# The keep and neg flags of a segment-maximum loop, loaded apart and the second one asked for three steps later

## The reference

```python
def _L2_gnn_ref(x, edge_index, edge_attr, W1, b1, W2, b2):
    rol, col = (edge_index[0], edge_index[1])
    e_feat = jnp.concatenate([x[rol], x[col], edge_attr], axis=-1)
    h = jax.nn.relu(e_feat @ W1 + b1)
    v = h @ W2 + b2
    x_cand = jax.ops.segment_max(v, col, num_segments=num_nodes)
    return jnp.maximum(x_cand, x[:, -v.shape[-1]:])
...
edge_index = jnp.stack([src, dst])
x = _layernorm(x + _L0_gnn_ref(x, src, dst, ...), axis=-1)
x = _layernorm(x + _L1_gnn_ref(x, edge_index, 3), axis=-1)
x = _layernorm(x + _L2_gnn_ref(x, edge_index, edge_attr_32, ...), axis=-1)
x = _layernorm(x + _L3_gnn_ref(x, edge_index), axis=-1)
```

## Time and profile before

| what | value |
|---|---|
| median of three runs | 13235.58 us |
| span of the profiled execution | 14030.5 us |
| the profiled execution's own time beside its span | not recorded, only the span is |
| the judging in it, 7445 to 12045 us | 4600 us |
| attention and count, 350 to 5270 us | 4920 us |
| two propagations, 5620 to 7300 and 12300 to 14030 us | 1680 and 1730 us |

### The profile page before, as it was taken

How to read it: one execution, slowest core, us unless ns; L and a number is a source line. 1 busy time by engine, 2 the same in 40 slices (tenths; PEclk the granted TensorE clock), 3 DMA queues, 4 the chain that set the end, 5 groups by cost and what they waited for, 6 DMA issues and landing times. The chain is left out here.

```text
span 14030.5 us, 252646 instructions
## 1 busy us (share of the span) xinstructions
PE 7954.3 (57%) x99382; PEld 6496.0 (46%) x99382; DVE 7349.7 (52%) x7867; ACT 4832.8 (34%) x7104; POOL 8433.5 (60%) x7325
## 2 busy tenths in 40 slices
PE   3455555555555554999872444434443443398988
PEld 2444444444444444989870111111111111298988
DVE  4566666666666665777761223222222222577777
ACT  1444444444444443656540000000000000165655
POOL 5777777777777773313246666666666666421323
PEclk7555555555555556999985666666666666699999
DMA  5233333323332335989871222222222222398988
GB/s 91 82 87 88 87 88 87 88 86 90 85 90 85 89 86 171 347 328 341 325 255 39 59 55 59 54 54 58 58 59 52 58 56 55 108 353 324 355 327 300
DMA packets 940767, 1950.86 MB, mean 139 GB/s; under 512 B 315485, under 2 KB 538547, under 8 KB 940331
## 3 DMA queue, kind: packets, MB, share of 16 engines
q1 hardware_dynamic: 587723, 1664.30, 32.6%
q0 software_dynamic: 235776, 185.47, 8.9%
q10 hardware_dynamic: 117216, 100.45, 2.6%
HBM read 1571.46 MB, written 381.38 MB: 139 GB/s over the span
## 5 line engine op out<-in xcount | busy, mean ns | idle before, releaser
L657 POOL DMA_INDIRECT attend_and_count_rows<-table,attend_and_count_ring x3136 | 3921.7, 1251 | 1073.4 <-issue 1001.7
L1353 POOL DMA_INDIRECT judge_edges_src_rows<-table,judge_edges_ring x3136 | 3029.0, 966 | 1535.5 <-issue 955.9
L692 PE MATMUL attend_and_count_counts<-attend_and_count_hot_hi,attend_and_count_hot_lo 128*128 128x98 bf16 x15680 | 1434.1, 269 | 2323.8 <-ACT attend_and_count_stage L801 1399.5
L1202 POOL DMA_INDIRECT base<-slot_sums,last_slot x588 | 976.0, 1660 | 2668.1 <-DMA slot_sums<-propagate_mean_whole 1236.7
L692 PEld LDWEIGHTS attend_and_count_counts<-attend_and_count_hot_hi,attend_and_count_hot_lo 128*128 128x128 bf16 x15680 | 1182.8, 132 | 2574.1 <-ACT attend_and_count_stage L801 1369.5
L801 ACT CAST attend_and_count_stage<-attend_and_count_counts 128x784 uint8<-128x784 f32 x1960 | 1533.5, 812 | 917.6 <-PE attend_and_count_counts L692 507.3
L1108 PE MATMUL propagate_mean_p_dense<-propagate_mean_split,propagate_mean_part 128*128 128x96 bf16 x36456 | 1647.2, 207 | 242.6 <-ACT propagate_mean_part L1015 171.0
L1108 PE MATMUL propagate_norm_p_dense<-propagate_norm_split,propagate_norm_part 128*128 128x96 bf16 x36456 | 1632.3, 206 | 246.4 <-ACT propagate_norm_part L1015 171.0
L1108 PEld LDWEIGHTS propagate_mean_p_dense<-propagate_mean_split,propagate_mean_part 128*128 128x128 f16 x36456 | 1621.1, 99 | 254.3 <-ACT propagate_mean_part L1015 171.1
L1108 PEld LDWEIGHTS propagate_norm_p_dense<-propagate_norm_split,propagate_norm_part 128*128 128x128 f16 x36456 | 1607.7, 99 | 257.1 <-ACT propagate_norm_part L1015 171.9
L1490 ACT ACTIVATE judge_edges_hidden<-judge_edges_p_hid,judge_edges_b 128x512 f32<-128x512 f32 x392 | 248.0, 685 | 4245.2 <-remote 3025.1
(11 more groups left out here) (264 smaller groups left out, 11991.4 us busy)
## 6 DMA issues: line engine op xcount, KB each, us to landing
propagate_mean_raw<-matrix SPq DMA_DIRECT2D x372, 1568.0 KB, 8.7
propagate_norm_raw<-matrix SPq DMA_DIRECT2D x372, 1568.0 KB, 8.6
matrix<-attend_and_count_stage SPq DMA_DIRECT2D x245, 784.0 KB
scan<-attend_and_count_out SPq DMA_DIRECT2D x196, 272.0 KB
inject<-attend_and_count_zeros SPq DMA_DIRECT2D x49, 1024.0 KB
attend_and_count_rows<-table,attend_and_count_ring POOLq DMA_INDIRECT x3136
judge_edges_src_rows<-table,judge_edges_ring POOLq DMA_INDIRECT x3136
judge_edges_dst_rows<-inject SPq DMA_DIRECT2D x195, 256.0 KB
```

What stands on the lines that cost most here:

```text
L657: nc.gpsimd.indirect_dma_start(out=rows[:, u, g, j, :], out_offset=None, in_=D.table0[:, :], in_offset=rows_of(ring[:, u, g, j:j + 1])).th ...
L692: last = nc.tensor.matmul(counts[:, r % 2, k // 4, NH * (k % 4):NH * (k % 4) + NH], hot_lo[:, u, slot, :], hot_hi[:, u, slot, :], start=Tr ...
L1202: nc.gpsimd.indirect_dma_start(out=sums[:, h, :], out_offset=None, in_=D.slot_sums[0:blocks * BLOCK, :], in_offset=rows_of(S.last_slot[:, ...
L1353: nc.gpsimd.indirect_dma_start(out=src_rows[:, u, lane, :], out_offset=None, in_=D.table2[:, :], in_offset=rows_of(ring[:, u, lane:lane + ...
```

## The change

`load_flags` is split into `load_keep` and `load_neg`. The `keep` load waits for `held` alone, the `neg` load for `topped` alone, and each has its own pair of semaphores. `keep` of steps h and h+1 is asked for where both were before, right after the row loads of step h. `neg` of the same two steps is asked for right after the row loads of step h+3; the last one after the last row loads. On DVE the scan over `keep` waits for the `keep` load, and the scan over `neg` has a wait of its own for the `neg` load. SP's list now has its first two turns written out, since the neg loads reach back into the turn before. Size, source, buffers and number of all transfers are the same.

```diff
--- before.py
+++ after.py
@@ -1284,7 +1284,8 @@
     listed = sem("judge_sources_listed")
     gathered = [sem(f"judge_rows{u}_gathered") for u in range(RING)]
     loaded = [sem(f"judge_edges{u}_loaded") for u in range(RING)]
-    flagged = [sem(f"judge_flags{b}_loaded") for b in range(2)]
+    keep_loaded = [sem(f"judge_keep{b}_loaded") for b in range(2)]
+    neg_loaded = [sem(f"judge_neg{b}_loaded") for b in range(2)]
     src_turned, edges_turned, spaced, held = (sem(f"judge_{what}") for what in (
         "sources_turned", "edges_turned", "firsts_turned", "dst_held"))
     lifted, rectified, sent = (sem(f"judge_{what}") for what in ("hidden_multiplied", "hidden_rectified", "messages_multiplied"))
@@ -1382,23 +1383,39 @@
                             sp.dma_start(of_quarters(rows[q * FEAT:q * FEAT + used, u]),
                                          along_quarters(edges, first, used)[q]).then_inc(loaded[u], 16)
 
-            def load_flags(it, b):
+            def flags_of_pair(kept, it, b):
+                of_each = kept[stretch(it * RING * CHUNK + 2 * b * CHUNK, (GROUPS - 1) * QUARTER + 2 * CHUNK)]
+                return bass.AP(of_each.tensor, of_each.offset, [[QUARTER, GROUPS], [0, FEAT], [1, 2 * CHUNK]])
+
+            def load_keep(it, b):
                 freed = awaited(sp, it * RING + (2 * b + 2 - RING))
                 sp.wait_ge(begun, 1)
                 await_count(sp, held, freed)
+                sp.dma_start(keep[:, 2 * b:2 * b + 2].rearrange("p s c -> p (s c)"), flags_of_pair(D.keep, it, b)).then_inc(keep_loaded[b], 16)
+
+            def load_neg(it, b):
+                freed = awaited(sp, it * RING + (2 * b + 2 - RING))
+                sp.wait_ge(begun, 1)
                 await_count(sp, topped, freed)
-                first = it * RING * CHUNK + 2 * b * CHUNK
-                for flags, kept in ((keep, D.keep), (neg, D.neg)):
-                    of_each = kept[stretch(first, (GROUPS - 1) * QUARTER + 2 * CHUNK)]
-                    of_each = bass.AP(of_each.tensor, of_each.offset, [[QUARTER, GROUPS], [0, FEAT], [1, 2 * CHUNK]])
-                    sp.dma_start(flags[:, 2 * b:2 * b + 2].rearrange("p s c -> p (s c)"), of_each).then_inc(flagged[b], 16)
+                sp.dma_start(neg[:, 2 * b:2 * b + 2].rearrange("p s c -> p (s c)"), flags_of_pair(D.neg, it, b)).then_inc(neg_loaded[b], 16)
 
             def one(it, u):
                 load(it, u)
                 if u % 2 == 0:
-                    load_flags(it, u // 2)
-
-            over_steps(sp, one)
+                    load_keep(it, u // 2)
+                elif not (isinstance(it, int) and it * RING + u == 1):
+                    ended, first = before(it, u, 3)
+                    load_neg(ended, first // 2)
+
+            for it in range(2):
+                for u in range(RING):
+                    one(it, u)
+            with sp.Fori(2, TURNS - 1) as it:
+                for u in range(RING):
+                    one(it, u)
+            for u in range(RING):
+                one(TURNS - 1, u)
+            load_neg(TURNS - 1, 1)
 
         @block.tensor
         def _(pe):
@@ -1447,7 +1464,7 @@
                 nc.vector.transpose(by_lane(attr_feat[:, u % 2]), attr_rows[:, u]).then_inc(edges_turned, 1)
                 await_count(dve, held, here)
                 nc.vector.transpose(by_lane(firsts[:]), dst_rows[:, u]).then_inc(spaced, 1)
-                dve.wait_ge(flagged[u // 2], it * 32 + 32)
+                dve.wait_ge(keep_loaded[u // 2], it * 16 + 16)
                 dve.wait_ge(spaced, here + 1)
                 nc.vector.tensor_tensor_scan(out=dst_feat[:, u % 2], data0=keep[:, u], data1=firsts[:],
                                              initial=dst_feat[:, 1 - u % 2, CHUNK - 1:],
@@ -1460,6 +1477,7 @@
                 dve.wait_ge(sent, here + 1)
                 await_count(dve, topped, here)
                 await_count(dve, back, here - 1)
+                dve.wait_ge(neg_loaded[u // 2], it * 16 + 16)
                 nc.vector.tensor_tensor_scan(out=best[:, u % 2], data0=neg[:, u], data1=p_msg[:, u % 2],
                                              initial=best[:, 1 - u % 2, CHUNK - 1:],
                                              op0=ALU.add, op1=ALU.max).then_inc(topped, 1)
```

## The result

The changed kernel takes 13304.59 us, the median of four runs (13296.33 to 13325.9), the kernel before 13236.4 us (four runs, 13234.04 to 13245.45). The ratio is 1.0055 with a 95% interval of 1.0040 to 1.0069: 68 us slower. I had forecast 13235 us and no change, and the end of my range was 13285. The profiled execution of the changed kernel took 13298.07 us, 1.8 us more than its span.

What follows compares the result with a forecast made beforehand. The prediction took POOL's gathers, 20.3 us a step, to set the judging's pace and hide every term, so the terms summed to 0 us and the forecast stayed at 13,235 us, range 12,840 to 13,285.

Steps and rivals of the forecast that it cites:

- the one on POOL: Judging stage: POOL's 3136 gathers and the gaps between them take 3984.9 us, which no flag can shorten.
- The flags' wait: DVE before the scan over keep: 97 waits, 722 us idle, vanish nearly whole; hidden by POOL, so worth 0.
- The row loads and the neg load: SP's list: row loads gain 0 by starting earlier; the later neg load is hidden by 31 us.
- this last wait: SP's wait for the scanned maxima, 1208.2 us in 49 pieces, should be gone.
- The added wait on DVE: One more semaphore before each of 196 scans of maxima: bounds 0 to 255 us, taken as nearly 0.
- Rival C: SP's list: keep still waits behind row loads, so the change does nothing; 13,235 us, counted within the forecast's 0.57.
- A burden of the profiled execution: Judging stage: late completions, some 57 us, and slow SP register moves occur in the profiled execution, not in timed runs.
- My sum over the stages: Of the profile's 794.9 us excess, 567.8 lie in the judging, leaving 227.1 us (2.4%) for other stages.
- the 567.8 us: Judging stage: POOL's 63 waits for ACT's copy of the indices, the most the change could gain; taken as absent from timed runs.
- Rival A: Judging: late completions are real, so removing flags' waits shortens POOL's waits by 397 to 567.8 us; chance 0.33.
- Rival B: SP's more frequent bursts delay PE's signals and add POOL waits: 57 to 284 us slower; chance 0.10.

Runs made afterwards that it cites:

- e9: Kernel before with keep and neg loads on separate signals, neg asked for where it was, plus a 128x768 DVE fill before the keep scan: 13348.88 us, 1.0078.
- e12: Kernel before with `firsts` in PSUM and nothing else, the flags' wait still in place: 13219.32 us, ratio 0.9984.
- e4: Changed kernel with `firsts` in PSUM, so the scan over keep has one SBUF input instead of two: 13222.6 us, ratio 0.9983.
- e5: Same edit as e9, on the chip where the kernel before takes 14008.75 us: 14024.2 us, ratio 1.0008.
- e8: Kernel before with `firsts` in PSUM (edit of e12), on the chip where the kernel before takes 14008.75 us: 14014.79 us, ratio 1.0002.
- e1: Kernel before, unchanged, run again for a second profiled execution: 13245.01 us, ratio 1.000.
- e6: Changed kernel with a 128x32 DVE fill before the scan over keep, on the chip where the kernel before takes 14008.75 us: 14015.71 us, ratio 1.0006.
- e7: Changed kernel with `firsts` in PSUM and a 128x768 fill before the keep scan, where the kernel before takes 14008.75 us: 14035.35 us, ratio 1.0014.
- e10: Changed kernel with a 128x32 DVE fill before the scan over keep in every step: 13274.24 us, ratio 1.0022.
- e13: Kernel before with the flags loaded in the first turn only (wrong flags later), SP's waits kept: 13267.98 us, ratio 1.0019.
- e11: Changed kernel with `firsts` in PSUM (e4) plus a 128x768 DVE fill before the scan over keep: 13223.85 us, ratio 0.9984.

## Why the prediction was wrong

**The step that failed** is the one on POOL: the 3984.9 us of gathers and gaps "can't be shortened by any flag", and "POOL's gathers stay at 3985 us with their gaps". I took a gather's duration for a constant, from a row that says otherwise: 942/947/1939 in the earlier trace rows has some gathers at twice the median, and 3029.0 us of the earlier trace rows less 3136 x 0.9445 = 2961.9 leaves 67 us that I didn't ask about. The right question was which gathers they are and what runs beside them. What the runs showed in its place: from the first gather to the last POOL takes 3934.9 us before, 4003.3 after and 3913.3 with no stretch at all. With POOL as the pace and DVE's scans moving against it, this was a term with a sign either way: e9 has 97 us of stretch more than the kernel before, e12 has 22 us less.

**What held.** The flags' wait is hidden by POOL and is worth 0: e4 and e12 differ by it and not in time. It did vanish (628.4 to 1.2 us). The row loads and the neg load cost nothing by coming late: no engine has a new wait for them, and SP now waits 1790.4 us for the scan over keep and 1459.6 for the maxima, where it waited 2971.7 for the maxima. I had said that this last wait should be gone. It is halved and not gone, since neg's wait is in the same queue. The added wait on DVE left no row. Rival C, that the change doesn't do what it says, is wrong: of 628.4 us 1.2 are left.

**"A burden of the profiled execution" is wrong.** The late signals are those of a kind of chip: on the chip of e5 to e8 the kernels take 14015 to 14035 us in timed runs and in profiled ones alike (e8: 14009.39 profiled, a median of 14014.79), and on the others a profiled execution is as fast as a timed one too (13298.07 beside 13296.33 to 13325.9). The first trace most likely came from such a chip, and the timed runs shown beside it from another; which chip they ran on isn't recorded, but the span, the wait for ACT and the register moves of SP (a median of 697 ns in the earlier trace rows, 698 in e8, 29 in e1) all fit. My sum over the stages pointed the right way, that the 567.8 us weren't in the timed runs, for a wrong reason. Against the trace of e1 the first one has 619 us more in the judging and 167 elsewhere, where I had reckoned 567.8 and 227.1. What makes PE's signals and SP's register moves late there is open.

**Rival A** is wrong even where its condition holds. On that chip e5, e6 and e7 have no flags' wait and gain none of the 397 to 567.8 us. The changed kernel itself wasn't run there; e6 comes nearest, with a fill that moves nothing in e10. The Trainium skill (Perfetto Trace Analysis, Optimization Strategy) advises to make earlier what the gaps of the most contended engine depend on. Where that engine has no gap that goes back to the flags (e4 against e12) nothing was gained, and here the side effect of the change on POOL's gathers cost 68 us.

**Rival B** had the sign, a time near the measured one (13,292 us with a tenth more waits, which is luck) and SP's bursts, but not the mechanism. There is no late completion in the changed kernel's profile, and POOL's wait for ACT didn't grow, it is 0. What the bursts moved is the landing of the gathers, by up to 2.8 us, and with it the phase of the scans. That half of the cause is shown by e13, the other half, the scan's second SBUF input, by e4, e11 and e12.

The version to keep is the kernel before or the changed one with `firsts` in PSUM (0.9984 and 0.9983). They are the same in time, and neither depends on a phase.

## What to carry to other kernels

Where the engine that sets the pace has a longest instruction of twice the median, find out what runs beside the long ones before costing anything else, because a change that moves only an idle engine can change their number. A wait of 600 us on an engine with slack may be worth nothing, and its removal may cost. And before a profiled span is compared with timed runs of another time, see that both are from a chip of the same kind: here the same program took 13245 us on one and 14009 on another.

## What the runs showed of the hardware

- A DVE scan of 128x512 with two inputs in SBUF holds up an indirect gather issued meanwhile on POOL until 0.75 us after the scan's end, by up to 1.0 us, and isn't slowed itself (1.28 us). With one input in PSUM it holds up none (the longest gather is 962 ns). With a fill of 128x768 right ahead of the scan the hold begins before the scan's own row and reaches 1.54 us (the longest gather of e9 is 2488 ns).
- Landing of a step's last gather (its start to the turning that waits for it): 2.3 to 2.4 us with SP's queue at rest or at the end of its burst, 3.1 to 4.1 in the last part of a burst of three, 5.1 amid its burst of six transfers, whose packets take 21 us.
- A fill of 128x32 (85 ns) behind the transposes moved the scan by nothing, one of 128x768 (698 ns) by 0.67 to 0.73 us.
- One kernel, two kinds of chip or states of one: 13243 to 13245 us on three chips and 14009 on a fourth. The second shows signals of PE that come late (waits of up to 44.8 us in e8), POOL waiting 618 us for ACT, and register moves of SP of 698 ns where they take 29 on the first.
